# Adding the two gated expert pairs on GpSimd before they are folded to tokens, in a two-layer vision tower

## The reference, cut to what matters

```python
topk_s, topk_i = jax.lax.top_k(scores, TOP_K)      # 2 of 4 experts
w = jax.nn.softmax(topk_s, axis=-1)
out = jnp.zeros_like(x)
for ei in range(NUM_EXPERTS):
    g = jnp.where(topk_i == ei, w, 0.0).sum(-1)
    hh = jax.nn.gelu(x @ W1[ei] + b1[ei], approximate=False)
    out = out + g[..., None] * (hh @ W2[ei] + b2[ei])
```

## Time and profile before

| | |
|---|---|
| time, median of 3 runs | 872.81 us (872.68 to 873.22) |
| time of the profiled execution | 871.04 us |
| its span, first to last instruction | 869.2 us |
| outside the span | 1.8 us |
| mean granted TensorE clock | 0.673 of full |
| `combine`: memset to the last `add` | 596.05 to 634.39 us |
| `ln2`: first statistics to the last copy | 635.46 to 651.2 us |

### The profile page before, as it was taken

The page is one execution under the profiler, slowest core; times in us unless marked ns, Lnnn a source line. Parts: engine busy times, 40 slices in busy tenths (PEclk is TensorE's granted clock), DMA queues, the critical chain, the costliest instruction groups (busy, mean ns, idle before and its releaser), DMA issues. The chain is left out here.

```text
span 869.2 us, 12176 instructions
## 1 busy us (share of the span) xinstructions
PE 575.1 (66%) x4215; PEld 346.1 (40%) x4215; DVE 579.1 (67%) x1309; ACT 267.6 (31%) x485; POOL 319.0 (37%) x373
## 2 busy tenths in 40 slices
PE   5517669756788859306766377624957772798886
PEld 4414446434466538203322233214935541522222
DVE  6985999999996472389876496566342438555453
ACT  1124223212222333013333042321043434545453
POOL 6013223122333402477777777700021110234334
PEclk9996655556688855556655565555557985589898
DMA  6100000000000000501111112000000000000001
GB/s 181 28 1 1 1 2 1 0 1 1 1 2 2 1 2 0 79 10 35 36 35 21 22 35 36 8 0 1 1 0 1 2 1 0 1 1 0 13 14 24
DMA packets 28633, 13.05 MB, mean 15 GB/s; under 512 B 22080, under 2 KB 25761, under 8 KB 28322
## 3 DMA queue, kind: packets, MB, share of 16 engines
q1 hardware_dynamic: 23842, 10.82, 5.2%
q0 software_dynamic: 4736, 1.51, 2.1%
HBM read 10.77 MB, written 1.54 MB: 14 GB/s over the span
## 5 line engine op out<-in xcount | busy, mean ns | idle before, releaser
L1453 POOL DMA_INDIRECT edge_scratch<-src_rows_dram,slot_src_index x144 | 156.7, 1088 | 46.7 <-issue 43.1
L599 POOL TENSOR_TENSOR wa_scores<-wa_scores,wa_max 128x512 f32<-128x512 f32 x32 | 37.1, 1160 | 163.5 <-DVE wa_max L780 163.5
L490 POOL TENSOR_TENSOR ln_xs<-xn,ln_stats 128x256 f32<-128x256 f32 x32 | 19.4, 615 | 154.8 <-DVE ln_stats L458 93.2
L644 PE MATMUL wa_s_ps<-wa_kbd,wa_qk 64*64 64x512 f32 x128 | 55.7, 960 | 29.8 <-issue 29.7
L543 PE MATMUL ln_pT<-ident,ln_xs 128*64 128x128 f32 (+1 forms) x112 | 28.0, 413 | 49.4 <-POOL ln_xs L490 48.7
L2054 POOL TENSOR_TENSOR moe_acc<-moe_acc,moe_weighted 128x512 f32<-128x512 f32 x28 | 37.7, 1347 | 49.7 <-DVE moe_weighted L1995 49.6
L1995 DVE SCALAR_TENSOR_TENSOR moe_weighted<-moe_y_ps,moe_b_cols,moe_G 128x512 f32<-128x512 f32 x32 | 24.0, 750 | 47.3 <-ACT moe_G L1968 43.9
L1574 PE MATMUL moe_h_ps<-xT,moe_w 65*128 65x512 f32 x64 | 54.1, 994 | 0.0
L737 ACT ACTIVATE wa_probsT<-wa_t_ps 128x512 f32<-128x512 f32 x32 | 19.1, 597 | 105.4 <-PE wa_t_ps L652 105.4
L1954 ACT ACTIVATE moe_hidden<-moe_h_ps,moe_b_cols 128x1024 f32<-128x1024 f32 x32 | 35.5, 1113 | 41.3 <-PE moe_h_ps L1886 41.3
L1894 PE MATMUL moe_y_ps<-moe_hidden,moe_w 128*64 128x512 f32 x128 | 39.0, 689 | 4.4 <-ACT moe_hidden L1954 2.3
(11 more groups left out here) (390 smaller groups left out, 1378.4 us busy)
## 6 DMA issues: line engine op xcount, KB each, us to landing
edge_onehot_T<-slot_lo_dram SPq DMA_DIRECT2D x16, 288.0 KB, 3.3
edge_scratch<-src_rows_dram,slot_src_index POOLq DMA_INDIRECT x144, 2.4
edge_scratch<-in_L_ffn_edge_index SPq DMA_DIRECT2D x2, 1024.0 KB, 6.3
xrow<-in_x SPq DMA_DIRECT2D x4, 256.0 KB, 7.8
out_h<-h SPq DMA_DIRECT2D x4, 256.0 KB, 2.6
moe_w<-in_L_ffn_W SPq DMA_DIRECT2D x3, 256.0 KB
src_rows_dram<-src_rows SPq DMA_DIRECT2D x1, 320.0 KB
moe_w<-in_L_ffn_W SPq DMA_DIRECT2D x2, 128.0 KB
```

The lines of the kernel that those rows point to most:

```text
L599: pool.tensor_tensor(sc[b][:], sc[b][:], bc(mx[b][:], WIN), ALU.subtract).then_inc(shifted, 1)
L644: ins = pe.matmul(s_ps[b][half], qk[b][half, 0, :], kbd[b][half])
L1453: pool.indirect_dma_start(gs[b][:, j, :], None, srow_dram, bass.IndirectOffsetOnAxis(edges.src_index[:, x:x + 1], axis=0))\
```

## The change

GpSimd adds the second gated pair to the first, in place (`tmp[0] += tmp[1]`, 128 x 512 float32), once per chunk, and counts a new semaphore `paired`. The fold waits for that semaphore and not for the multiplies, and folds one sum: four matmuls a chunk, none of which accumulates.

```diff
+    paired = mem.sem("gate_pairs_added")
     with nc.Block() as block:
         @block.gpsimd
         def _(pool):
             pool.memset(parts[:, :, :, E0:E1], 0.0).then_inc(zeroed, 1)
+            for c in range(n):
+                pool.wait_ge(gated, 2 * c + 2)
+                first, second = tmp[0][c % 2][:], tmp[1][c % 2][:]
+                pool.tensor_tensor(first, first, second, ALU.add).then_inc(paired, 1)
...
             def fold(c):
-                pe.wait_ge(gated, 2 * c + 2)
+                pe.wait_ge(paired, c + 1)
                 if c > 1:
                     pe.wait_ge(added, c - 1)
                 for t in range(4):
-                    for p in range(2):
-                        ins = pe.matmul(f_ps[c % 2][:, t, :], tmp[p][c % 2][:, t * P:(t + 1) * P], k.fold[:],
-                                        start=p == 0, stop=p == 1)
+                    ins = pe.matmul(f_ps[c % 2][:, t, :], tmp[0][c % 2][:, t * P:(t + 1) * P], k.fold[:])
                 ins.then_inc(folded, 1)
```

## The result

| | kernel before | changed kernel |
|---|---|---|
| median of 19 runs | 868.99 us (864.63 to 875.95) | 860.29 us (853.35 to 869.52) |
| ratio to before | | 0.9876, 95% interval 0.9849 to 0.9903 |
| profiled execution, its span | 871.04, 869.2 us | 860.29, 858.4 us |
| mean granted TensorE clock | 0.673 | 0.681 |

The changed kernel is faster by 1.24% with an interval of 0.97 to 1.51%, or 0.0124 x 868.99 = 10.8 us (8.4 to 13.1). The forecast was 863.4 us, 9.4 less than 872.8 (1.08%), with a range from 859.4 to 867.0.

The account below looks back on a forecast made before the run. TensorE, mostly its folds, was taken to bound `combine`. Passes -13.7, start +4.2, end +0.9 and `ln2` -0.8 gave -9.4 us, so 872.8 - 9.4 = 863.4 us, range 859.4 to 867.0.

Parts of the forecast that it names:

- Fewer passes: Folds of `combine`: 64 of 128 TensorE passes go, 0.214 us each, 13.7 us less; period from 4.48 to 2.77 us.
- The price of one addition: GpSimd in `combine`: 1.27 us per addition, sum ready 2.62 us after the fold's first load, wanted after 2.77.
- The formula for the period: Steady part of `combine`: (2.69 + 1.29 + 0.08 + P + 0.06) / 2 for addition P; passes 2.77 us at P = 1.42.
- The end: Last fold of `combine`: no gates ahead, TensorE wants the sum after 1.71 us, ready after 2.62; costs 0.91 us.
- The start: First fold of `combine`: GpSimd's configuration and first addition delay it from 600.60 to 604.76 us, 4.16 us lost.
- `ln2`: Start of `ln2`: with the configuration done earlier, scalings start sooner; 0.8 us comes back, bounds 0 to 1.17.
- The sum: Whole kernel: -13.7 (passes) + 4.2 (start) + 0.9 (end) - 0.8 (`ln2`) = -9.4 us.
- Contention in `combine`: Rival, chance 0.15: GpSimd and VectorE slow each other; additions of 1.64 us give 864.7 us, stretched products too 869.5.
- No exposed configuration: Rival, chance 0.09: configuration over before the first products, fold begins at 601.95, 861.4 us in all.
- The clock up in `combine`: Rival, chance 0.08: TensorE's granted clock rises in the stage, period near 2.1 us, 859.4 us in all.
- The clock down behind it: Rival, chance 0.06: second attention loses its high TensorE clock; 25 us of loss costs 17 us, 880.6 us in all.
- The page's figure: Start of `combine`: the skill's 5.95 us for a first GpSimd call, against the row's 6.9; start 0.95 us earlier.

Follow-up runs that it names:

- the second one: The changed kernel timed again beside the version with early configuration and pairs on VectorE: ratio 0.9888 to the kernel before, median 860.99 against 871.44 us.

## Why the prediction was right, and where it was off

- **Fewer passes, 13.7 us: right.** The period of the steady part is 2.77 us, to the digit, and the experiment with the passes put back returned it to 4.47.
- **The price of one addition, 1.27 us, hidden by 0.15: right.** All eight took 1.25 to 1.27 us. The formula for the period, (4.12 + P) / 2, gave 3.36 on average for a doubled addition; the run shows 2.72 and 3.95, mean 3.34, and the last `add` at the forecast 34.6 us.
- **The end, 0.9 us: right.** The wait is 0.78 us.
- **The start, 4.2 us: right.** The configuration was the hidden term: with it out of the way the first fold came 2.7 us earlier. The time from it to the first use was put at 5.7 to 6.9 us, and the sum took 6.9. In `combine` it was 6.7, 7.0 and 7.5 us in three profiles of the changed kernel, so the first fold came 8.5, 8.8 and 9.3 us after the memset, where 8.7 was expected. That is 3.9, 4.3 and 4.8 us lost, 4.3 in the mean; that the forecast meets this to 0.1 us is in part luck, with a spread of 0.8.
- **`ln2`, 0.8 us: right.** Its first scaling comes 1.5 us earlier. The third comes 9.31 us after the last `add` (637.43 - 628.12) instead of 10.26 (644.65 - 634.39), 0.95 us earlier, and VectorE's subtraction beside the first two scalings did take 1.02 us, as forecast. Of the 0.95 us, 0.33 is a shorter way through the barrier, which I had not seen: VectorE's first instruction waits 0.32 us for it, and in the kernel before it waited 0.65:

```profile
635.46 0.69 DVE L442 TENSOR_REDUCE ln_stats<-h 128x8 f32<-128x512 f32 x1 [0.65 <-PEq L1759]
```

  It was 0.65 in the three profiles that have the configuration in `ln2`, and 0.32 in the nine that don't. The rest is 0.62, the figure that the forecast had worked out. To ia the stage gives back 0.9 us at one clock, and between -0.2 and 1.0 by single pairs of profiles.
- **The sum: right.** Memset to ia is 57.9 and 57.3 us in two profiles before, 48.1, 49.0 and 49.3 in three after, by the means 57.6 - 48.8 = 8.8 us less, against 9.4 forecast. The 57.3 is the profile with the higher clock in `ln2`; with the 57.9 alone it is 9.1. The two profiles that stand at the head of this document differ by 9.8. The last `add` was expected 29.7 us after the memset and came at 29.5, 29.8 and 30.3. The timings give 10.8 (8.4 to 13.1) and, in the second one, 0.0112 x 871.44 = 9.8 us.
- **The level: the step that failed.** The forecast of 863.4 us was 872.8 - 9.4, and the 872.8 was the median of three runs. Over 19 runs the kernel before has 868.99 us, 3.8 us lower. The changed kernel's median of 860.29 lies at the lower end of the range, and what the ratio makes of the 868.99, 858.2 us (855.9 to 860.6), lies 1.2 us under it. With the level put right the same sum gives 868.99 - 9.4 = 859.6 us, inside that interval. The range was made of the mechanism's terms alone and held nothing for the starting level. The spread of single runs, 864.6 to 876.0, is larger than the terms that I weighed; three runs that agree within 0.5 us did not show it, though the profiled execution, 1.8 us below them, was a hint that I used only as an offset. The 1.7 us that a measurement was said to tell was small too: the interval here is 2.3 us either way.
- **The rivals.** Contention in `combine`: none. The additions took 1.27 us beside VectorE's `add`, which alone runs beside them for more than 0.1 us in the changed kernel, and the same beside the products in the run with the second pair added twice; both read one input from PSUM. The Trainium skill (GPSIMD Engine Reference, "Key points") names contention with VectorE instructions that have two SBUF inputs or run in a 2-port mode. The trace agrees on the first: the subtraction in `ln2`, with both inputs in SBUF, took 1.02 us beside GpSimd's scalings and 0.69 without. No exposed configuration: refuted here, and made true by the experiment that moved it. The clock up in `combine`: no, 0.50 throughout. The clock down behind it: no; ia to the second mixture took 99.6 us in both profiles of the first pair, at a clock of 0.74 in both. That TensorE's clock moves the later stages by several us is true, but the same holds for the kernel before against itself.
- **The page's figure.** The Trainium skill (GPSIMD Engine Reference, "Instruction dispatch") measured 5.95 us. The runs show 5.6 to 6.0 us ahead of the all-reduce, which agrees, and 6.7 to 7.8 us ahead of a `TENSOR_TENSOR`; the choice to go by the row was the better one.

## What to carry to other kernels

Look in the instruction order for what a new instruction drags along: in this kernel the first `TENSOR_TENSOR` on GpSimd behind an all-reduce brings a configuration of some 7 us that shows in no busy time, and a two-column dummy placed in an idle stretch took it off the path. To see whether work on another engine is hidden, follow the chain from the fold that frees a buffer to the fold that needs it, over as many chunks as there are buffers, and not the load of the engine. Where single runs spread by more than the effect, anchor a forecast on the ratio and not on a level from three runs, read experiments by stage, and compare stages at the same granted clock.

## What the runs showed of the hardware

The time from MODIFY_POOL_CONFIG to the first use of what it loads was 5.6 to 6.0 us ahead of an all-reduce (5.7 in the first profile), and ahead of a `TENSOR_TENSOR` 6.7 to 7.8 us (6.7 to 7.5 in `combine`; 7.2 to 7.8 at the end of the router; 6.9 to 7.1 in `ln2`). It ran while the instruction behind it still waited for its semaphore: in `combine` it began at 599.1, the product was there at 603.13, and the addition started at 605.82. The memset of `combine` ran ahead of it, at 598.63. The same addition of two 128 x 512 float32 tiles in SBUF takes 1.27 us on GpSimd and 0.69 us on VectorE. The second mixture needed 110.5 to 115.6 us with the same instructions, at a granted clock of 0.92 down to 0.85.
